# A Fourier tower's column transform with the data as stationary operand, its modes copied by ScalarE, layer 0 as a loop, and the ends of the layers in another order

## The chip, the cores and the metric

The kernel runs on one core of one Trainium2 chip. The metric is the device time of the whole program in microseconds, the median of several executions. The engines of the core are TensorE (PE: matmuls; PEld: its weight loads), VectorE (DVE), ScalarE (ACT), GpSimd (POOL) and SyncE (SP, which here only issues DMAs).

## The reference, cut to what matters

64 images of 64 x 64 tokens pass through a Fourier tower of four layers with 32 channels, then an attention block and a mixture of experts. The change touches the tower alone:

```python
x = coords @ fc0_w + fc0_b                       # 3 -> 32 channels
for sw, cw, cb in layers:                        # four layers
    x_ft = rfft2(x, norm='ortho')
    out = einsum('bixy,ioxy->boxy', x_ft[:, :, :20, :20], sw)   # 20 x 20 modes
    x1 = irfft2(out in a zeroed spectrum)
    x2 = einsum('bchw,oc->bohw', x, cw) + cb
    x = gelu(x1 + x2)
x = gelu(x @ fc1_w + fc1_b) @ fc2_w + fc2_b
```

## The kernel before, in words

The Fourier transforms are matmuls with small constant matrices, all in fp32. The images go through a layer in 32 pairs (`PAIRS`). For pair j of layer l, TensorE runs `step(l, j)`, in this order:

- `inverse_h(l, j + 1)` (line 541): the inverse column transform of the next pair, 8 matmuls of 64 x 64 weights and 320 columns, into PSUM banks 4 to 7;
- `conv(l, j)` (line 563): the 1 x 1 convolution, 16 matmuls of 32 x 32 and 512 columns, into banks 0 to 3;
- `inverse_w(l, j, 0)` (line 579): half of the inverse row transform, 32 matmuls of 64 x 64 and 64 columns, added onto banks 0 and 1;
- `dft_w` of pair j - 2 of the next layer (line 474): the forward row transform, 16 matmuls of 32 x 64 and 512 columns, into banks 4 to 7;
- `inverse_w(l, j, 1)`: the other half, onto banks 2 and 3;
- `dft_h` of pair j - 3 of the next layer (line 486): the forward column transform, 8 matmuls of 64 x 64 and 320 columns, into banks 0 and 1. Here the constant `fwd_h` is stationary and the data `turned_h` moves.

An fp32 matmul runs as two passes, each with a weight load and a matmul of its own in the trace, so 8 matmuls are 32 instructions. VectorE turns 32 x 32 blocks between the transforms: `turn_inverse` (line 776, two transposes of 1024 elements), `turn_act` (line 741, two), `turn_w` (line 752, two), `turn_modes` (line 766, one of 640) and `turn_h` (line 758, one of 640: out of `dft_h`'s banks into `modes`). That is also their order within a step: `turn_inverse(j + 1)`, `turn_act(j - 1)`, `turn_w(j - 2)`, `turn_modes(j + 3)`, `turn_h(j - 3)`. ScalarE applies the GELU to each half of the convolution's banks (line 890) and issues the store of the pair to HBM. SP loads the pair back for the next layer.

Banks 4 to 7 are used by `inverse_h` and by `dft_w`, so in each step `inverse_h`, `turn_inverse`, `dft_w` and `turn_w` follow one another, and the next `inverse_h` waits for `turn_w` (`take(w_turned, ...)`). `conv` waits for `turn_h` of pair j - 4, which frees banks 0 and 1.

Waits of TensorE inside a loop can only be on constants, so `steps` runs two steps a round and then takes off what the semaphores gained:

```python
with pe.Fori(0, rounds):
    for j in range(first, first + 2):
        step(l, j)
    for sem, count in used:
        give_back(sem, count)        # pe.nop().then_inc(sem, -count), line 460
```

`used` has nine semaphores in layers 1 and 2 and five in layer 3. Layer 0 is written out (`looped = 0`); in layers 1 and 2 pairs 4 to 29 run in 13 rounds. The line of the loop itself is 615.

After the last pair of a layer come the forward transforms still open (`ends`), with a few idle matmuls (`keep_busy`, line 569) between them, and then `mix(l)` (line 527), which multiplies all modes with the layer's spectral weights; it needs every pair's modes. Layer 0's spectrum is not made from the 32 channels but from the four input channels: for four groups of eight pairs, `dft_w`, `dft_h` and `turn_h` work on the input, and `lift` (line 504, copies on ScalarE at line 869) spreads it to the channels. Layer 0's convolution reads the input, which SP loads in four pieces of 1 MB (`xin`), with weights in `first_w`.

## Time and profile before

| | us |
|---|---|
| median of 3 executions | 1547.61 |
| lowest, highest | 1542.99, 1552.35 |
| the profiled execution | 1544.01 |
| its span on the core | 1542.2 |
| TensorE, weight loads, VectorE, ScalarE busy | 1369.6, 704.4, 1181.8, 532.8 |
| the tower's layers: first inverse transposes of layers 0, 1, 2, 3 | 65.67, 363.64, 660.58, 954.54 |

The busy time of TensorE counts each matmul from its start to a modelled end; several run side by side on tiles of the array, and the groups give the time in which at least one ran. An idle time stands before the group that ended it, with what released it; "issue" is time in which TensorE waited for nothing that the profile shows. The granted clock was the full one (1.00, 2.4 GHz) in all stretches of the pair loops.

### The profile page before, as it was taken

The page shows a single profiled execution, that of the slowest core. Times are in us where ns is not written, and L with a number is a line of the kernel's source. Part 1 is how long each engine was busy: PE and PEld are TensorE (multiplying, and loading weights), DVE is VectorE, ACT ScalarE, POOL GpSimd, SP SyncE. Part 2 cuts the span into 40 slices and gives each one's busy share as a digit, 9 for nine tenths or more (in the row PEclk, how much of TensorE's full clock was granted, in tenths as well). Part 3 has the DMA queues.
Part 4 walks back from the last instruction along what each step waited for, and adds up shares of the span by engine and source line. Part 5 has one row for each costly group of instructions (what it writes and reads, how often), then busy time and mean ns, then how long its engine had stood idle before and what let it go on. Part 6 is the DMA issues. An engine that isn't in the chain of part 4 may idle for free. (4 is left out here: it accounts for less than half of the span.)

```text
span 1542.2 us, 69028 instructions
## 1 busy us (share of the span) xinstructions
PE 1369.6 (89%) x32216; PEld 704.4 (46%) x32216; DVE 1181.8 (77%) x1433; ACT 532.8 (35%) x673; POOL 92.4 (6%) x45
## 2 busy tenths in 40 slices
PE   8888999997999999879999998778779998989996
PEld 3544444445444444544444445445531117853332
DVE  4499999997999999789999997555510007878886
ACT  2422222223222222222222222333359994421221
POOL 1000000000000000000000000000000000036551
PEclk9999999999999999999999999999999999999998
DMA  6324242346666666566666663899997751056420
GB/s 230 115 115 164 116 163 119 133 166 224 249 247 244 249 241 255 177 255 246 245 245 245 245 250 130 311 372 387 375 377 278 280 190 59 8 129 152 116 76 14
DMA packets 59934, 315.80 MB, mean 205 GB/s; under 512 B 16704, under 2 KB 18688, under 8 KB 25984
## 3 DMA queue, kind: packets, MB, share of 16 engines
q1 hardware_dynamic: 36512, 177.95, 34.0%
q10 hardware_dynamic: 23264, 135.49, 21.4%
q8 instruction: 130, 2.13, 0.6%
q14 instruction: 28, 0.23, 0.1%
HBM read 176.05 MB, written 137.36 MB: 203 GB/s over the span
## 5 line engine op out<-in xcount | busy, mean ns | idle before, releaser
L890 ACT ACTIVATE act_c<-slots,conv_b 128x1024 f32<-128x1024 f32 x256 | 282.1, 1115 | 717.8 <-PE slots L579 717.8
L776 DVE STREAM_TRANSPOSE inv_out<-slots 128x1024 f32<-128x1024 f32 x256 | 304.7, 1229 | 96.7 <-PE slots L541 96.7
L579 PEld LDWEIGHTS slots<-inv_w,inv_out 64*64 64x64 f32 x16384 | 270.7, 136 | 198.9 <-issue 188.7
L579 PE MATMUL slots<-inv_w,inv_out 64*64 64x64 f32 x16384 | 301.6, 224 | 14.7 <-issue 9.6
L752 DVE STREAM_TRANSPOSE turned_h<-slots 128x1024 f32<-128x1024 f32 x200 | 238.0, 1229 | 24.5 <-PE slots L474 24.4
L474 PE MATMUL slots<-turned_w,fwd_w 32*64 32x512 f32 x3200 | 201.5, 599 | 28.7 <-DVE inv_out L776 22.1
L741 DVE STREAM_TRANSPOSE turned_w<-act_c 128x1024 f32<-128x1024 f32 x192 | 225.6, 1218 | 0.8 <-ACTq L893 0.8
L541 PE MATMUL slots<-turned_k,inv_h 64*64 64x320 f32 x2048 | 169.3, 444 | 53.7 <-DVE turned_h L752 30.4
L563 PE MATMUL slots<-xin,conv_w 32*32 32x512 f32 x3072 | 112.7, 605 | 29.3 <-DMA xin<-act_scratch 17.6
L486 PE MATMUL slots<-turned_h,fwd_h 64*64 64x320 f32 x1600 | 132.7, 443 | 1.3 <-DVE turned_h L752 1.3
L541 PEld LDWEIGHTS slots<-turned_k,inv_h 64*64 64x64 f32 x2048 | 71.0, 133 | 131.1 <-DVE turned_h L752 76.5
L474 PEld LDWEIGHTS slots<-turned_w,fwd_w 32*64 32x64 f32 x3200 | 69.3, 131 | 90.1 <-issue 87.2
L766 DVE STREAM_TRANSPOSE turned_k<-modes 128x640 f32<-128x640 f32 x128 | 102.9, 807 | 0.5
L1781 POOL TENSOR_TENSOR modes<-at_turned,modes 128x1024 f32<-128x1024 f32 x6 | 14.4, 2394 | 1375.2 <-DMA at_turned<-level_scratch 1367.1
L901 ACT ACTIVATE inv_out<-slots,b 128x512 f32<-128x512 f32 x86 | 89.7, 1111 | 2.1 <-PE slots L698 2.1
L758 DVE STREAM_TRANSPOSE modes<-slots 128x640 f32<-128x640 f32 x96 | 77.5, 809 | 2.3 <-PE slots L486 2.3
L850 DVE TENSOR_SCALAR modes<-slots,b 128x512 f32<-128x512 f32 x4 | 3.0, 751 | 95.9 <-PE slots L710 95.9
L698 PE MATMUL slots<-act_c,w 32*64 32x512 f32 x1024 | 71.4, 612 | 3.9 <-ACT inv_out L901 1.8
L486 PEld LDWEIGHTS slots<-turned_h,fwd_h 64*64 64x64 f32 x1600 | 52.1, 132 | 35.4 <-issue 5.4
L563 PEld LDWEIGHTS slots<-xin,conv_w 32*32 32x32 f32 x3072 | 24.3, 103 | 80.5 <-DVE modes L758 34.9
L527 PE MATMUL slots<-modes,mode_w 64*64 64x128 f32 x1600 | 49.8, 271 | 6.3 <-issue 5.2
L800 DVE COPY modes<-slots 128x640 f32<-128x640 f32 x36 | 29.7, 825 | 33.2 <-PE slots L527 33.2
(166 smaller groups left out, 1116.8 us busy)
## 6 DMA issues: line engine op xcount, KB each, us to landing
act_scratch<-act_c ACTq DMA_DIRECT2D x128, 1024.0 KB, 4.2
xin<-act_scratch SPq DMA_DIRECT2D x96, 1024.0 KB, 4.8
act_c<-act_scratch SPq DMA_DIRECT2D x32, 1024.0 KB, 6.1
mode_w<-in_sw_dram SPq DMA_DIRECT2D x20, 640.0 KB, 4.3
at_turned<-level_scratch SPq DMA_DIRECT2D x24, 256.0 KB, 4.2
at_ret_t<-level_scratch SPq DMA_DIRECT2D x20, 256.0 KB, 4.2
xin<-in_x_dram SPq DMA_DIRECT2D x4, 1024.0 KB, 8.6
turned_w<-in_x_turned_dram SPq DMA_DIRECT2D x3, 1024.0 KB, 5.4
```

The costliest lines, as they stand in the source:

```text
L474: mm = nc.tensor.matmul(banks[i * 64:(i + 1) * 64, 4 + p, :], fwd_w[p * 32:(p + 1) * 32, wh, :], turned_w[p * 32:(p + 1) * 32, n % 2, wh, ...
L486: mm = nc.tensor.matmul(banks[kwh * 64:(kwh + 1) * 64, at + i, 0:320], fwd_h[i * 64:(i + 1) * 64, parity, ph, :], turned_h[i * 64:(i + 1) ...
L541: mm = nc.tensor.matmul(banks[s * 64:(s + 1) * 64, 4 + 2 * i + kwh, 0:320], inv_h[rows, l % 2, s * 64:(s + 1) * 64], turned_k[rows, t % 2, ...
L563: nc.tensor.matmul(banks[q * 32:(q + 1) * 32, p, :], w, src, start=True, stop=False, skip_group_check=True)
L579: mm = nc.tensor.matmul(banks[half * 64:(half + 1) * 64, 2 * two + odd, at:at + 64], inv_out[rows, t % 2, i, two, s, 2 * half:2 * half + 2 ...
L741: last = nc.vector.transpose(dst, src)
L752: nc.vector.transpose(dst, src).then_inc(w_turned, 1)
L758: nc.vector.transpose(dst, src).then_inc(modes_set, 1)
L766: nc.vector.transpose(dst, src).then_inc(modes_turned, 1)
L776: nc.vector.transpose(dst, src).then_inc(inv_turned, 1)
L890: nc.scalar.activation(act_c[:, t % RING, :, at, :].rearrange("p i q m -> p q i m"), banks[:, at, :].rearrange("p q (i m) -> p q i m", i=2 ...
L901: nc.scalar.activation(unit[n % 3][:, part, :], banks[:, at, :], ACT.Gelu, bias=b1[:, 0:1]).then_inc(unit_set, 1)
```

## The change

1. `dft_h` turns its operands round: the data (`turned_h`, 128 rows by 64 columns) is loaded as weights and the constant moves, 40 columns at a time. The constant now holds all 128 rows. The result comes out with the modes along the free dimension, so that it need not be transposed but only copied.
2. That copy is ScalarE's (`copy_modes`), behind the pair's second GELU and ahead of the store's issue; `turn_h` is gone from VectorE. At the start, `copy_first` is a copy on VectorE.
3. The layout of the modes changes with it: `mix_place` sets where each mode of the mixing goes, `inverse_h` becomes 16 matmuls of 32 x 64 weights and 320 columns that add up in pairs, `turn_inverse` reads all four banks for each image, and `lift` runs as 2 matmuls of 64 x 64 instead of 4 of 32 x 32. Host-made constants and the order of the spectral weights follow. The bytes loaded stay the same.
4. Layer 0 is looped like the others: the input comes in a piece for each pair (`load_x`, four DMAs of 32 KB), and `first_w` is the same for every pair. In layers 0 to 2 the loop runs over pairs 5 to 30.
5. At a layer's end `dft_w` of pair 29 comes ahead of the last `conv`; the last pair's activation is turned in two halves (`turn_last_act`), the first as soon as the first GELU is done; the last `dft_w` goes into banks 0 to 3 and the last two `dft_h` into banks 4 and 5 and 6 and 7.

```diff
@@ dft_w, dft_h
-            def dft_w(n):
+            def dft_w(n, at=4):
...
-                            mm = nc.tensor.matmul(banks[i * 64:(i + 1) * 64, 4 + p, :],
+                            g = i ^ p % 2
+                            mm = nc.tensor.matmul(banks[g * 64:(g + 1) * 64, at + 2 * i + p // 2, :],
...
-                for ph in range(2):
-                    take(w_turned, after_w_turned(n, ph))
-                    for i in range(2):
+                for i in range(2):
+                    take(w_turned, after_w_turned(n, i))
+                    for b in range(MIXES // 2):
                         for kwh in range(2):
-                            mm = nc.tensor.matmul(banks[kwh * 64:(kwh + 1) * 64, at + i, 0:320],
-                                                  fwd_h[i * 64:(i + 1) * 64, parity, ph, :],
-                                                  turned_h[i * 64:(i + 1) * 64, n % 2, ph,
-                                                           kwh * 320:(kwh + 1) * 320].rearrange(
-                                                      "p (b c m) -> p b m c", c=CH, m=2),
-                                                  start=(ph == 0), stop=(ph == 1))
+                            at_kw = kwh * 320 + b * 64
+                            mm = nc.tensor.matmul(
+                                banks[kwh * 64:(kwh + 1) * 64, at + i, b * 40:(b + 1) * 40],
+                                turned_h[:, n % 2, i, at_kw:at_kw + 64],
+                                fwd_h[:, i, parity, :].rearrange("p (k x) -> p k x", k=2)[:, :, 0:MODES],
+                                start=(b == 0), stop=True, skip_group_check=True)
@@ inverse_h
-                for i in range(2):
+                for odd in range(2):
                     for s in range(2):
-                        for kwh in range(2):
-                            rows = slice(kwh * 64, (kwh + 1) * 64)
-                            mm = nc.tensor.matmul(banks[s * 64:(s + 1) * 64, 4 + 2 * i + kwh, 0:320],
-                                                  inv_h[rows, l % 2, s * 64:(s + 1) * 64],
-                                                  turned_k[rows, t % 2, i * 320:(i + 1) * 320],
-                                                  start=True, stop=True)
+                        for r in range(4):
+                            rows = slice(r * 32, (r + 1) * 32)
+                            mm = nc.tensor.matmul(
+                                banks[s * 64:(s + 1) * 64, 4 + r, :].rearrange("p (i n) -> p i n", i=2)[:, :, 0:160],
+                                inv_h[rows, l % 2, odd, s * 64:(s + 1) * 64],
+                                turned_k[rows, t % 2, odd * 320:(odd + 1) * 320].rearrange("p (i n) -> p i n", i=2),
+                                start=(odd == 0), stop=(odd == 1))
@@ step
+                final = j == PAIRS - 1 and not last
+                if final:
+                    take(act_turned, after_turn(l + 1, j - 2))
+                    take(w_turned, after_w_turned(forward(l + 1, j - 3), 1))
+                    dft_w(forward(l + 1, j - 2))
@@ the layers of TensorE
-                first = 1 if last else 4
-                looped = 2 * ((PAIRS - 1 - first) // 2) if l > 0 else 0
+                first = 1 if last else 5
+                looped = 2 * ((PAIRS - 1 - first) // 2)
...
-                    dft_w(ends[1])
-                    take(act_high, after_set(l, PAIRS - 1))
-                    keep_busy(4, 3)
-                    dft_h(ends[0], parity, at=2)
-                    take(act_turned, after_turn(l + 1, PAIRS - 1))
-                    take(w_turned, after_w_turned(ends[1], 1))
-                    dft_w(ends[2])
-                    take(modes_set, ends[0])
-                    dft_h(ends[1], parity)
-                    take(modes_set, ends[0] + 1)
-                    dft_h(ends[2], parity, at=2)
-                    keep_busy(2, 4)
+                    dft_w(ends[2])
+                    take(act_low, after_set(l, PAIRS - 1))
+                    dft_h(ends[0], parity)
+                    take(act_high, after_set(l, PAIRS - 1))
+                    dft_h(ends[1], parity, at=2)
+                    take(act_turned, after_turn(l + 1, PAIRS - 1))
+                    take(modes_set, ends[1] + 1)
+                    dft_w(ends[3], at=0)
+                    dft_h(ends[2], parity, at=4)
+                    keep_busy(4, 7)
+                    dft_h(ends[3], parity, at=6)
+                    keep_busy(2, 0)
@@ VectorE
-                    if 3 <= j < PAIRS - 1:
-                        turn_h(forward(l + 1, j - 3), modes[:, 2 * (j - 3):2 * (j - 3) + 2])
                 if not last:
-                    turn_act(l + 1, PAIRS - 1)
+                    turn_last_act(l + 1)
                     turn_w(forward(l + 1, PAIRS - 2))
-                    for t in range(PAIRS - 4, PAIRS):
-                        if t == PAIRS - 2:
-                            turn_w(forward(l + 1, PAIRS - 1))
-                        turn_h(forward(l + 1, t), modes[:, 2 * t:2 * t + 2],
-                               at=2 if t in (PAIRS - 3, PAIRS - 1) else 0)
+                    turn_w(forward(l + 1, PAIRS - 1), at=0)
@@ ScalarE
+            def copy_modes(f, t, at=0):
+
+                act.wait_ge(h_done, forward(f, t) + 1)
+                nc.scalar.copy(modes[:, 2 * t:2 * t + 2, :, 0:MODES], modes_from(at)).then_inc(modes_set, 1)
...
+                        if two == 0 and t == PAIRS - 1 and l < LAYERS - 1:
+                            act.drain().then_inc(act_half, 1)
                     act.drain().then_inc(act_ready, 1)
+                    if t >= 3 and l < LAYERS - 1:
+                        copy_modes(l + 1, t - 3)
                     act.dma_start(act_dram[t], flat(act_c[:, t % RING])).then_inc(act_stored[t % RING], 16)
+                if l < LAYERS - 1:
+                    for t in range(PAIRS - 3, PAIRS):
+                        copy_modes(l + 1, t, at=2 * (t - PAIRS + 4))
@@ SP
+            def load_x(t):
+
+                if t >= IN_RING:
+                    sp.wait_ge(summed, after_out(0, t - IN_RING, 0))
+                for p in range(4):
+                    sp.dma_start(flat(xin[p * CH:p * CH + IN_CH, t % IN_RING]), x[t, p]).then_inc(
+                        xin_in[t % IN_RING], 16)
```

## Rows read from the trace of the kernel before

**Rows 1.** The page: span, busy time, the layers' GELUs.

```profile
PE 1369.6 (89%) x32216; PEld 704.4 (46%) x32216; DVE 1181.8 (77%) x1433; ACT 532.8 (35%) x673; POOL 92.4 (6%) x45
...
L890 ACT ACTIVATE act_c<-slots,conv_b 128x1024 f32<-128x1024 f32 x256 | 282.1, 1115 | 717.8 <-PE slots L579 717.8
```

**Rows 2.** Timeline, layer 1, one loop turn (start, us, engine, line, op).

```profile
504.39 1.31 PE L541 MATMUL slots<-turned_k,inv_h 64*64 64x320 f32 x16 [0.28 <-DVE turned_h L752]
504.99 0.81 DVE L758 STREAM_TRANSPOSE modes<-slots 128x640 f32<-128x640 f32 x1
505.76 2.38 DVE L776 STREAM_TRANSPOSE inv_out<-slots 128x1024 f32<-128x1024 f32 x2
...
508.07 2.34 DVE L741 STREAM_TRANSPOSE turned_w<-act_c 128x1024 f32<-128x1024 f32 x2
...
508.29 1.98 PE L474 MATMUL slots<-turned_w,fwd_w 32*64 32x512 f32 x32 [0.17 <-DVE inv_out L776]
...
510.20 1.05 PEld L579 LDWEIGHTS slots<-inv_w,inv_out 64*64 64x64 f32 x64 [0.81 <-issue]
...
510.36 2.38 DVE L752 STREAM_TRANSPOSE turned_h<-slots 128x1024 f32<-128x1024 f32 x2
511.15 0.78 PEld L486 LDWEIGHTS slots<-turned_h,fwd_h 64*64 64x64 f32 x16
...
513.04 1.31 PE L541 MATMUL slots<-turned_k,inv_h 64*64 64x320 f32 x16 [0.52 <-DVE turned_h L752]
...
514.41 2.38 DVE L776 STREAM_TRANSPOSE inv_out<-slots 128x1024 f32<-128x1024 f32 x2 [0.21 <-PE slots L541]
```

**Rows 3.** VectorE's timeline: inverse-transform transposes of layers 0 and 1.

```profile
133.08 2.38 DVE L776 STREAM_TRANSPOSE inv_out<-slots 128x1024 f32<-128x1024 f32 x2
...
142.87 2.38 DVE L776 STREAM_TRANSPOSE inv_out<-slots 128x1024 f32<-128x1024 f32 x2 [0.21 <-PE slots L541]
...
201.74 2.38 DVE L776 STREAM_TRANSPOSE inv_out<-slots 128x1024 f32<-128x1024 f32 x2
...
403.42 2.38 DVE L776 STREAM_TRANSPOSE inv_out<-slots 128x1024 f32<-128x1024 f32 x2
...
608.08 2.38 DVE L776 STREAM_TRANSPOSE inv_out<-slots 128x1024 f32<-128x1024 f32 x2
```

**Rows 4.** TensorE's sequencer at that loop turn: line 460.

```profile
L460 PEldq EVENT_SEMAPHORE  x9: 51/51/51, 511.2 to 512.4; - x9
```

**Rows 5.** Begun before a stretch's end: lines 579, 486 (PE, PEld xcount).

```profile
510.19:510.94 0.75, 0.75 (x48) 0.75 (x52) 1.00 1.00 426
...
510.94:511.18 0.24, 0.00 (x0) 0.03 (x4) 1.00 0.73 308
```

**Rows 6.** Timeline, later stage: loads of 128 rows by 64 columns.

```profile
1382.21 0.20 PEld L1267 LDWEIGHTS slots<-at_qkv,ex_lattice_w 128*64 128x64 f32 x4 [0.37 <-issue]
...
1383.12 0.14 PEld L1267 LDWEIGHTS slots<-at_centred_y,ex_lattice_w 128*64 128x64 f32 x2 [0.28 <-issue]
```

**Rows 7.** PE groups by form after 960 us: 128*128 and 128*64 forms.

```profile
L1210 PE MATMUL slots<-at_qkv,at_ret_t 128*128 128x64 f32 x64 | 7.9, 276 | 1.6 <-DVE at_ret_t L1418 1.6
```

**Rows 8.** DMA queue of instructions: 100 to 200 us, 400 to 500 us.

```profile
q8 instruction: 21, 0.34, 1.4%
...
q8 instruction: 2, 0.03, 0.2%
```

**Rows 9.** Timeline: end of layer 0 and start of layer 1's mixing.

```profile
326.50 2.38 DVE L752 STREAM_TRANSPOSE turned_h<-slots 128x1024 f32<-128x1024 f32 x2
...
336.26 2.33 DVE L741 STREAM_TRANSPOSE turned_w<-act_c 128x1024 f32<-128x1024 f32 x2
...
341.00 1.54 DVE L758 STREAM_TRANSPOSE modes<-slots 128x640 f32<-128x640 f32 x2
...
347.50 11.96 PE L527 MATMUL slots<-modes,mode_w 64*64 64x128 f32 x392 [0.33 <-DVE modes L758]
```

**Rows 10.** ScalarE's groups by form: the lift's copies.

```profile
L869 ACT COPY modes<-slots 128x400 f32<-128x400 f32 x32 | 15.8, 492 | 21.3 <-PE slots L504 21.3
```

More of the change, by code:

```diff
@@ L501, in lift @@
                     pe.wait_ge(first_w_set, 1)
-                for b in range(4):
-                    rows_b = slice(b * 32, (b + 1) * 32)
-                    mm = nc.tensor.matmul(banks[rows_b, 2 + n % 2, 0:400], lift_w[rows_b, e, :],
-                                          in_modes[rows_b, 2 * q:2 * q + 2, :, 0:MODES], start=True, stop=True)
+                for kwh in range(2):
+                    rows = slice(kwh * 64, (kwh + 1) * 64)
+                    mm = nc.tensor.matmul(banks[rows, 2 + n % 2, 0:400], lift_w[rows, e, :],
+                                          in_modes[rows, 2 * q:2 * q + 2, :, 0:MODES], start=True, stop=True)
                 mm.then_inc(lifted, 1)
@@ L629, in _ @@
             pe.wait_ge(fc0_cols_set, 1)
-            for e in range(LIFT_E):
-                mm = nc.tensor.matmul(banks[:, 3, e * CH:(e + 1) * CH], fc0_cols[:, e, :], conv_w[0:CH, 0, :],
-                                      start=True, stop=True)
-            mm.then_inc(first_w_filled, 1)
+            nc.tensor.matmul(banks[:, 3, 0:CH], fc0_cols, conv_w[0:CH, 0, :],
+                             start=True, stop=True).then_inc(first_w_filled, 1)
             warm_up(1)
@@ L714, in _ @@
             for _ in range(4):
-                nc.tensor.matmul(banks[:, 0, 0:128], inv_h[:, 0, :], inv_h[:, 0, :], start=True, stop=True)
+                nc.tensor.matmul(banks[:, 0, 0:128], inv_h[:, 0, 0, :], inv_h[:, 0, 0, :], start=True, stop=True)
         def mix_part(u, side, images=slice(0, IMAGES)):
-            k, half = u // 2 * 2 + side, u % 2
+            k, half = mix_place(u, side), u % 2
             dst = modes[:, images, k, half * 10:half * 10 + 10].rearrange("p i (m r) -> p i m r", r=2)
@@ L1825 @@
     fc0 = _np.concatenate([f[t + "fc0_w"], f[t + "fc0_b"][None, :]], axis=0)
+    for m in range(2):
+        lifted[:, :, :, m, :, m] = fc0
     wq, wk = f["L0_attn_W_Q"], f["L0_attn_W_K"]
```

153 lines of the change are left out of this document (87 added, 66 removed).

## The prediction

> **What bounds the kernel now.** The page first: TensorE is busy 89% of the span and VectorE 77%, ScalarE 35% [rows 1]. Both leaders are averages, so I went to the timeline of the pair loop, where layers 0 to 2 spend some 250 us each. One step there is a ring of four pieces that hand PSUM banks 4 to 7 to each other [rows 2]: `inverse_h` starts at 504.39; its two transposes (line 776) start 1.37 later, at 505.76, and last 2.38; `dft_w` follows at 508.29, that is 3.90 after the start, and lasts 1.98; its transposes (line 752) start at 510.36 and end at 512.74. If the next `inverse_h` came 0.05 later, the step would be 8.40 us. That is what layer 0, written out, shows: 142.87 to 201.74 is 7 steps, 8.41 each [rows 3]. VectorE's own list of a step comes to the same 8.41, since it has no gap in layer 0. So two limits of one size lie on each other, VectorE's list and the bank ring, and taking work from one alone wins nothing.
>
> In layers 1 and 2 TensorE runs a loop of two steps, and the mean is (608.08 - 403.42) / 24 = 8.53 [rows 3]: 8.41 and 8.65 in turn. The longer one is the loop's turn: `inverse_h` starts at 513.04, 0.30 after its transposes ended [rows 2]. The sequencer shows why. `give_back` makes nine semaphore decrements, the first at 511.2, 0.15 apart, then comes the branch, and the matmul starts 1.86 after the first decrement (511.18 to 513.04) [rows 2, 4]. When can that first decrement start? When line 579's half had 48 matmuls and 52 loads of 64 and 64 begun, the sequencer reached the wait behind it: 28 instructions stood queued. When `dft_h` had 4 loads of its 32 instructions begun, the first decrement came: 28 again [rows 5]. So the sequencer is held until the last 28 instructions before it are queued, and the decrements start only then. With today's `dft_h` that is right at its beginning.
>
> **The change part by part.** `dft_h` was 8 matmuls of 320 columns (16 loads and 16 matmuls, because each runs in two passes); it becomes 20 of 40 columns with 128 rows, so 40 loads and 40 matmuls on two column tiles. The trace has no such form. A second load on the same 128 by 64 tile comes 0.06 after the first (four loads in 0.20, two in 0.14) [rows 6], and line 579 with 16 loads on each of four tiles takes (1.05 - 0.14) / 15 = 0.06 a round [rows 2]. Twenty rounds make 1.21 us, against 1.31 for the 320-column form of the same size [rows 2]. The array's time hardly changes. The lower bound is line 579's rate over all tiles, 0.016 for each load, so 0.66; the upper one is that the two tiles don't run side by side, 2.42. I take 1.21, from the row with the same tile.
>
> The loop's turn pays. `dft_h` now has 80 instructions, and the first decrement must wait until 52 have gone: 52/80 of 1.21 = 0.79 after its first load. That load comes 3.90 + 1.91 + 0.95 = 6.76 after the step's start (508.29, 510.20, 511.15) [rows 2], and later by a change of tile shape, which was not there: 1.98 for 2048 columns and 1.31 for 1280 give 0.87 ns a column, so 1.79 for `dft_w`, while its successor starts after 1.91. I take 0.13 (bounds 0 and 0.2). Then 6.76 + 0.13 + 0.79 + 1.86 = 9.54 instead of 8.65: **+0.89 a turn**. Three layers have 13 rounds each: 39 x 0.89 = +34.7. The lower bound of the round gives 26 loads x 0.016 = 0.43, so +0.53 a turn and +20.7. In the other step `dft_h` ends at 6.76 + 0.18 + 1.21 + 0.17 (a last matmul's way out) = 8.32, just under the 8.40 of the ring; its cost there is nothing, but only 0.08 covers it.
>
> On the number queued, the trace shows 28 both times [rows 5]. The Trainium skill, "TensorE: Matmul & The Clock Gate", section Part 1, has TensorE's queue 64 deep; no row here shows that many waiting. By its 64 the turn would grow by 0.37 instead of 0.89; that case is a rival below.
>
> On loads: line 1210 has full 128-row loads, 64 of them with their matmuls in 7.9 us, 0.123 each [rows 7], less than a 128-column load at 0.06 for 64 (0.12) and 64 columns of matmul (0.05) one after the other. The same page, Part 3, says that a load overlaps a running matmul only where the row groups differ; by that `dft_h` would be serial, about 3.7 us, and the step longer than 10. The row of line 1210 speaks against it here.
>
> `inverse_h` becomes 16 matmuls on eight tiles with the same columns for each tile. `dft_w`, which has eight tiles, ends no later for it than the columns say; I take +0.02 on the ring for each of 93 steps, +2 (bounds 0 and 0.06 each). Waits and order of it are unchanged.
>
> Layer 0 becomes a loop. It gets 13 turns it did not have: 13 x 0.24 = +3.1 beside the 0.89 counted. It loses its three code stalls: 133.08 to 142.87 is 9.79 instead of 8.41 [rows 3], and two more of the kind cost 1.07 and 1.38: -3.8. The instruction queue fetched 21 times in 100 us of layer 0 and twice in 100 us of layer 1 [rows 8]. The input comes in four small DMAs a pair instead of a megabyte per eight pairs; each has two steps, 16.8 us, to land, and SP has nothing else to issue: nothing.
>
> The transpose of line 758, 0.81, leaves VectorE, 29 a layer in the stream [rows 2]. What hides it is the ring's 8.40; price nothing. VectorE then idles 0.7 a step while `inverse_h` runs. The end of a layer: from the end of line 752's transposes, 326.50 + 2.38 = 328.88, to mixing at 347.50 is 18.6 [rows 9]. Up to the last pair's turn (336.26) that was 7.4; with `dft_w` first it is 2.1 + conv 1.1 + two halves 2.2 + the last GELU 1.1 [rows 1] and handovers 0.2 = 6.7. From there it was 11.2; now a half turn 1.2 and a transposed pair 2.4, beside them two `dft_h` (2.5) and ScalarE's copies; `dft_w` into banks 0 to 3 ends 6.1 after the turn's start, its transposes at 8.5, the last half of `dft_h` 9.2, the copy 9.7. That is -0.7 - 1.5 = -2.2 a layer, -6.6 (bounds -3 and -10, for code stalls that move).
>
> ScalarE's copy of 400 elements takes 0.49, the lift's form [rows 10]. In the stream it starts once `dft_h` ends, 8.4, and ends at 8.9; `conv`, which waits for it, comes at 9.7. Behind it on ScalarE stand the store's issue, which is read a layer later, and a GELU due at 10.9: nothing. At the start four transposes become copies, at most 0.3 shorter each, partly hidden: -0.5; the wider lift weights fill an idle VectorE.
>
> Sum: +34.7 + 3.1 - 3.8 + 2.0 - 6.6 - 0.5 = **+28.9** on the profiled execution's 1544.0, so 1572.9; the median shown, 1547.6, is 3.6 higher, and I give 1576.
>
> **The rivals.** (a) The loop's turn does not lengthen, because the decrements start beside `dft_h` as they do now. Then only +3.1 - 3.8 + 2.0 - 6.6 - 0.5 = -5.8: 1542; with the smallest `inverse_h` and other code stalls gone too, 1536. This is the only way to faster, and it decides at the first decrement: it must stay within 0.1 of `dft_h`'s first load. The 28 queued speak against it; for it speaks that VectorE's list gets 9% shorter. 0.27, half of it faster. (b) The sequencer can run further ahead than the 28 seen, by 64: then 16 instructions of `dft_h` must be gone, 4 rounds, 0.24, so +0.37 a turn, 14.4 in all, and 1556. 0.09. (c) The two tiles of 128 rows don't run side by side: `dft_h` 2.42, the plain step 9.5, the turn 10.3, some +110: 1657. Against it speaks that two loads of this tile pair begin together [rows 6]. 0.05. (d) The loop's body, 528 instructions a step where it was 448, no longer stays in the instruction buffer and is fetched at each of 39 turns for about 1.2 us (the stalls of layer 0), +47: 1623. 0.06.
>
> **How the numbers follow.** The forecast has 0.53 with its own range 1560 to 1592, from the bounds of the round and of the ends. About 0.5% is what a measurement of this kernel tells from no change, 1540 to 1555. Faster is half of (a), 0.13; same the other half and little of (b), 0.14; slower 0.73. For 8 in 10, 1541 to 1602 leaves out part of (a), (c) and (d).
>
> **What would show it.** The loops' steps alternate 8.4 and 9.5; in the turn, the first decrement of line 460 comes 0.8 after `dft_h`'s first load; 28 instructions are queued then; `dft_h` lasts about 1.35; VectorE idles 0.7 a step; layer 0 has no code stall and the period of layers 1 and 2; each layer's end is 2 us shorter. If the turn stays at 8.65, the step on the queue is wrong, and the result is (a). If the plain step is over 8.5, the round is longer than 0.06.

## The result, and the profile after

The changed kernel takes 1610.3 us (1602.1 to 1614.8) where the kernel before took 1550.0 on the same chip: ratio 1.039, 95% interval 1.033 to 1.045, so +60 us. The forecast was 1576, range 1541 to 1602. The direction was right, and the time lies 8 us above the range. The profiled execution after takes 1610.4; that of before was a quick one (1544.0), so the two traces differ by 66 us, 6 more than the medians.

The page after (the span and busy rows, then the rows that answer to [rows 1] and the groups of the changed operations; lines 503, 516, 570, 593, 609 are `dft_w`, `dft_h`, `inverse_h`, `conv` and `inverse_w`, lines 773, 798, 811 and 821 `turn_act`, `turn_w`, `turn_modes` and `turn_inverse`, line 556 `mix`, line 911 `copy_modes`, line 488 `give_back`):

```profile
span 1608.6 us, 77928 instructions
PE 1418.4 (88%) x36522; PEld 826.4 (51%) x36522; DVE 1113.8 (69%) x1355; ACT 580.3 (36%) x769; POOL 92.3 (6%) x45
...
q8 instruction: 96, 1.57, 0.4%
...
L931 ACT ACTIVATE act_c<-slots,conv_b 128x1024 f32<-128x1024 f32 x256 | 282.2, 1114 | 714.2 <-PE slots L609 713.8
...
L570 PE MATMUL slots<-turned_k,inv_h 32*64 32x320 f32 x4096 | 182.5, 447 | 75.0 <-DVE turned_k L811 43.0
...
L516 PE MATMUL slots<-fwd_h,turned_h 128*64 128x40 f32 x4000 | 137.1, 230 | 3.5 <-issue 3.5
...
L911 ACT COPY modes<-slots 128x400 f32<-128x400 f32 x96 | 47.2, 492 | 41.8 <-PE slots L516 41.8
```

VectorE lost 68 us of work, as meant, and TensorE gained 49. To see where the time went, the two traces are cut at the same events: the first and the tenth inverse transpose (line 776 before, line 821 after) of a layer, its last one, and the first matmul of the mixing. The forecast is cut the same way from its own terms (it counts a turn's 0.89 or 1.13 in the stretch in which the turn lies):

| stretch, us | before | after | difference | forecast |
|---|---|---|---|---|
| start to the mixing of layer 0 | 47.8 | 50.4 | +2.6 | -0.5 |
| the four mixings, first matmul to first inverse transpose | 66.1 | 75.7 | +9.6 | 0 |
| first to tenth inverse transpose, layers 0, 1, 2 | 67.4, 65.5, 65.3 | 71.9, 77.0, 77.1 | +27.8 | +3.0 |
| tenth to last, layers 0, 1, 2 | 188.8, 187.5, 187.4 | 197.3, 198.5, 198.8 | +30.9 | +29.5 |
| last to the next mixing, three ends | 25.6, 27.7, 25.5 | 25.4, 24.4, 24.4 | -4.7 | -3.1 |
| from layer 3's first inverse transpose on | 587.7 | 587.7 | 0 | 0 |

The loops, the ends and the last layer came as priced. Two stretches did not: the mixing, which the forecast did not look at, and the first nine steps of a layer, most of which are written out. The timeline of one loop turn after, layer 1 (start, us, engine, line, operation), against [rows 2]:

```profile
500.34 1.19 PE L609 MATMUL slots<-inv_w,inv_out 64*64 64x64 f32 x64
...
501.46 1.25 PEld L516 LDWEIGHTS slots<-fwd_h,turned_h 128*64 128x64 f32 x40
501.46 1.36 PE L516 MATMUL slots<-fwd_h,turned_h 128*64 128x40 f32 x40
...
503.91 1.46 PE L570 MATMUL slots<-turned_k,inv_h 32*64 32x320 f32 x32 [1.09 <-DVE turned_k L811]
...
505.45 2.38 DVE L821 STREAM_TRANSPOSE inv_out<-slots 128x1024 f32<-128x1024 f32 x2 [1.84 <-PE slots L570]
...
507.98 1.98 PE L503 MATMUL slots<-turned_w,fwd_w 32*64 32x512 f32 x32 [0.39 <-DVE inv_out L821]
...
510.05 2.38 DVE L798 STREAM_TRANSPOSE turned_h<-slots 128x1024 f32<-128x1024 f32 x2
511.01 1.25 PEld L516 LDWEIGHTS slots<-fwd_h,turned_h 128*64 128x64 f32 x40
511.01 1.36 PE L516 MATMUL slots<-fwd_h,turned_h 128*64 128x40 f32 x40
...
512.42 0.49 ACT L911 COPY modes<-slots 128x400 f32<-128x400 f32 x1 [0.15 <-PE slots L516]
512.49 1.34 PE L570 MATMUL slots<-turned_k,inv_h 32*64 32x320 f32 x32
```

At 501.46 `dft_h` starts; `inverse_h` comes 2.45 later, at 503.91, though its banks were free at 502.88 (line 798 from 500.50 for 2.38). That is 1.03 behind the banks, where the plain step's `inverse_h` is 0.06 behind them (512.49 against 510.05 + 2.38): the turn is 0.97 late, and the rest of its extra 1.1 is the longer `inverse_h` (1.46 instead of 1.34). In the plain step `dft_h` (511.01 + 1.36 = 512.37) is done 0.12 before the ring lets `inverse_h` start, at 512.49. From 503.91 to 512.49 is 8.58, the step after a turn; the transposes of line 821 stand 8.48 and 9.6 apart in turn. The sequencer's decrements of that turn (count, ns, first and last start):

```profile
L488 PEldq EVENT_SEMAPHORE  x9: 51/51/51, 502.1 to 503.3; - x9
```

And `dft_h`'s matmuls and loads begun up to the first of them:

```profile
core 0: us, PE busy (x) PEld busy (x), PEclk, DMA share, GB/s
501.45:502.08 0.63, 0.62 (x22) 0.62 (x22) 1.00 1.07 455
```

The first comes 0.62 after `dft_h`'s first load, with 22 loads and 22 matmuls of 80 begun: 36 stand queued, not the 28 of [rows 5]. From it to `inverse_h` are 1.83, as before (1.86).

### The profile page after: what moved, and what is told of

It is laid out like the page before. It is cut to its first block and busy times, and to the rows that moved or that the text cites. A ratio compares the mean times of both kernels' runs of the same rounds, so it can differ in the third digit from the quotient of the medians.

```text
span 1608.6 us, 77928 instructions
## 1 busy us (share of the span) xinstructions
PE 1418.4 (88%) x36522; PEld 826.4 (51%) x36522; DVE 1113.8 (69%) x1355; ACT 580.3 (36%) x769; POOL 92.3 (6%) x45
## 5 line engine op out<-in xcount | busy, mean ns | idle before, releaser
L570 PE MATMUL slots<-turned_k,inv_h 32*64 32x320 f32 x4096 | 182.5, 447 | 75.0 <-DVE turned_k L811 43.0
L503 PE MATMUL slots<-turned_w,fwd_w 32*64 32x512 f32 x3200 | 206.9, 606 | 44.6 <-DVE inv_out L821 31.9
L773 DVE STREAM_TRANSPOSE turned_w<-act_c 128x1024 f32<-128x1024 f32 x186 | 218.7, 1216 | 0.0
L570 PEld LDWEIGHTS slots<-turned_k,inv_h 32*64 32x64 f32 x4096 | 88.6, 133 | 110.6 <-PEq L488 43.9
L516 PE MATMUL slots<-fwd_h,turned_h 128*64 128x40 f32 x4000 | 137.1, 230 | 3.5 <-issue 3.5
L516 PEld LDWEIGHTS slots<-fwd_h,turned_h 128*64 128x64 f32 x4000 | 125.4, 138 | 18.5 <-issue 12.5
L593 PE MATMUL slots<-xin,conv_w 32*32 32x512 f32 x3072 | 113.5, 605 | 19.5 <-DMA xin<-act_scratch 17.7
L556 PE MATMUL slots<-modes,mode_w 64*64 64x128 f32 x1600 | 64.9, 300 | 0.6 <-issue 0.6
L556 PEld LDWEIGHTS slots<-modes,mode_w 64*64 64x64 f32 x1600 | 63.9, 136 | 1.8 <-issue 1.3
L911 ACT COPY modes<-slots 128x400 f32<-128x400 f32 x96 | 47.2, 492 | 41.8 <-PE slots L516 41.8
```

The lines of the kernel that those rows point to most:

```text
L503: mm = nc.tensor.matmul(banks[g * 64:(g + 1) * 64, at + 2 * i + p // 2, :], fwd_w[p * 32:(p + 1) * 32, wh, :], turned_w[p * 32:(p + 1) * 3 ...
L516: mm = nc.tensor.matmul(banks[kwh * 64:(kwh + 1) * 64, at + i, b * 40:(b + 1) * 40], turned_h[:, n % 2, i, at_kw:at_kw + 64], fwd_h[:, i, ...
L556: mm = nc.tensor.matmul(mix_sums(rows_to, side, u % 2)[:, m * 128:(m + 1) * 128], mode_w[rows, n % RING_W, side, kh, :], modes[rows, :, k, ...
L570: mm = nc.tensor.matmul(banks[s * 64:(s + 1) * 64, 4 + r, :].rearrange("p (i n) -> p i n", i=2)[:, :, 0:160], inv_h[rows, l % 2, odd, s * ...
L593: nc.tensor.matmul(banks[q * 32:(q + 1) * 32, p, :], w, src, start=True, stop=False, skip_group_check=True)
L773: last = nc.vector.transpose(dst, src)
```

## The experiments

The table names three suspects: the loop turn, the mixing, and code that comes late in the written-out steps. On the last of them two theories stood. **A**: 528 instructions a step come too slowly whenever they run for the first time, whatever the traffic. **B**: they come late only beside the activations' megabyte transfers. The first seven kernels take one part out of the changed kernel or put one part into the kernel before. In several of them the numbers computed are not the transform's; they are for timing alone. Each ratio is to the kernel before, timed again beside that run (1547.2 to 1550.3); differences in us are between medians, and are good to some 5 to 10.

**dft_h_back**: the changed kernel with `dft_h` of 8 matmuls of 320 columns.

```diff
-                    for b in range(MIXES // 2):
+                    for r in range(2):
                         for kwh in range(2):
...
-                                turned_h[:, n % 2, i, at_kw:at_kw + 64],
-                                fwd_h[:, i, parity, :].rearrange("p (k x) -> p k x", k=2)[:, :, 0:MODES],
...
+                                fwd_h[r * 64:(r + 1) * 64, i, parity, :],
+                                turned_h[r * 64:(r + 1) * 64, n % 2, i, kwh * 320:(kwh + 1) * 320]...,
...
```

> The changed kernel with dft_h back at 8 matmuls of 64x64 weights and 320 columns; everything else of the change stays (the modes that come out are not the transform's). Theory (the queue before the loop's turn): the turn falls from 9.5 us to about 8.65, 39 of them, some -34 us, and the code stalls of the written-out steps shrink too, since a step has 48 instructions fewer; 1550 to 1570 in all. Rival (dft_h costs nothing, all of the loss is in the mixing and the code stalls): over 1595, the turn stays near 9.5.

Measured 1572.9 us, ratio 1.016 (1.010 to 1.021), 3 above the range expected. The steps of layers 1 and 2 are 8.48 and 8.71; tenth to last transpose takes 190.7, 189.1 and 188.9 instead of 197.3, 198.5 and 198.8, so 26 us come back there, and 15 in the first nine steps. `dft_h`'s new form is the larger half of the loss (37 of 60 us).

**dft_h_alone**: the kernel before with 20 such matmuls of 64 columns in `dft_h`.

```diff
-                    for i in range(2):
+                    for b in range(MIXES // 2):
                         for kwh in range(2):
...
-                                                  fwd_h[i * 64:(i + 1) * 64, parity, ph, :],
-                                                  turned_h[i * 64:(i + 1) * 64, n % 2, ph, ...
...
+                                turned_h[:, n % 2, ph, at_kw:at_kw + 64],
+                                fwd_h[:, parity, ph, :],
...
```

> The kernel before with dft_h alone in the new form: 20 matmuls with 128x64 weights from the data, 64 columns each here so that turn_h finds its banks filled (the values are not the transform's). Layer 0 stays written out. Theory (the sequencer's nine decrements start only once most of dft_h has gone): 26 turns at 9.4 to 9.5 us instead of 8.65, plain steps at 8.41 to 8.5, some +22 us, and code stalls on top in written-out steps, above all layer 0's 32: 1575 to 1610. Rival (dft_h's array time is what costs): plain steps grow too, by over 0.3 us each.

Measured 1568.1, ratio 1.010 (1.006 to 1.015), less than the 1575 to 1610 expected. Steps 9.43 and 8.41 in layers 1 and 2, where the loop is, and mostly 8.41 in layer 0, where there was none, though `dft_h` lasts 1.39 there: its array time costs nothing, the turn pays. Layer 0's stalls grow a little (tenth to last transpose 193.5 against 188.8). At the turns 34 instructions stand queued.

**inverse_h_alone**: the kernel before with `inverse_h` of 16 matmuls.

```diff
-                for i in range(2):
+                for odd in range(2):
                     for s in range(2):
-                        for kwh in range(2):
-                            rows = slice(kwh * 64, (kwh + 1) * 64)
-                            mm = nc.tensor.matmul(banks[s * 64:(s + 1) * 64, 4 + 2 * i + kwh, 0:320],
...
+                        for r in range(4):
+                            rows = slice(r * 32, (r + 1) * 32)
+                            mm = nc.tensor.matmul(banks[s * 64:(s + 1) * 64, 4 + r, :]...[:, :, 0:160],
...
```

> The kernel before with inverse_h alone as 16 matmuls of 32x64 weights (values not the transform's). Theory: it ends 0.03 later and lies on the ring of banks 4 to 7, so plain steps take 8.44 to 8.48 instead of 8.41, +3 to +7 us. Rival: hidden, no change.

Measured 1565.0, ratio 1.010 (1.008 to 1.013): +16, where 3 to 7 were expected. The plain step is 8.47, so `inverse_h` costs the ring 0.06, my upper bound, not 0.02. The rest is not the ring's: the first nine steps of a layer lose 8.6 us in the trace (206.8 for three layers, against 198.2), most of it in stalls of written-out steps, which have 32 instructions more. A turn grows to 8.7 or 8.96; in such a one it also lasts 1.59, where the plain step has 1.34. Its timeline, a turn and a plain step:

```profile
506.51 1.59 PE L541 MATMUL slots<-turned_k,inv_h 32*64 32x320 f32 x32 [0.53 <-DVE turned_h L753]
...
515.23 1.34 PE L541 MATMUL slots<-turned_k,inv_h 32*64 32x320 f32 x32 [0.28 <-DVE turned_h L753]
```

**mix_undone** (places and targets of the mixing as before), **mix_tiles** (the targets alone) and **mix_alone** (the kernel before with the changed places and targets). The change had put into `mix`:

```diff
+            block, odd = (2 * (u // 4) + side, u // 2 % 2) if u < 8 else (4, side)   # mix_place
+            return 2 * block + odd
...
-                                to = kwh ^ side
-                                k, kh = u // 2 * 2 + side, u % 2 * 5 + m
+                                k, kh = mix_place(u, side), u % 2 * 5 + m
+                                to = kwh ^ k // 2 % 2
```

In steps 8 and 9 `k // 2 % 2` is 0 for both sides, so their matmuls use two of the four 64 by 64 tiles. In steps 0 to 7 all four are used, but the two sides read modes two places apart, not side by side.

> The changed kernel with the mixing's places as before: the two sides read neighbouring places (k, k+1), and all ten steps use four tiles (the modes then belong to other weights). Theory (the mixing lost its speed by where the two sides read and by the two-tile steps): a mixing step takes 1.10 to 1.27 us again instead of 1.45 and 2.18, some -4 us a layer, 1590 to 1597. Rival (the mixing waits for the copies or for its code): the steps stay at 1.45, no change from 1610.

> The changed kernel with only the tiles of the mixing's last two steps as before, four instead of two. If the two-tile steps alone were the loss, all of -16 us comes back; the theory says that only their part does: 2.18 to about 1.2 us for two steps a layer, -8 us at most, and the eight others stay at 1.45 us, since their two sides read places two apart.

> The kernel before with the changed kernel's places and tiles in the mixing alone (modes then meet other weights). Theory: mixing steps 1.45 and 2.18 us instead of 1.10 to 1.27, +16 us. Rival (the slower mixing came from another part of the change): no change.

Measured: mix_undone 1598.3, ratio 1.032 (1.024 to 1.040); mix_tiles 1604.1, 1.035 (1.029 to 1.041); mix_alone 1558.3, 1.006 (1.003 to 1.008). The intervals are wide for differences of 6 to 12 us; the traces are sharper. Per layer the mixing lasts 18.9 in the changed kernel and in mix_alone, 16.9 in mix_tiles, and 15.7 to 16.8 in mix_undone. VectorE's copies behind the last four steps of the mixing, layer 1, changed kernel:

```profile
374.38 0.82 DVE L844 COPY modes<-slots 128x640 f32<-128x640 f32 x1 [0.62 <-PE slots L556]
375.84 0.82 DVE L844 COPY modes<-slots 128x640 f32<-128x640 f32 x1 [0.63 <-PE slots L556]
378.00 0.82 DVE L844 COPY modes<-slots 128x640 f32<-128x640 f32 x1 [1.34 <-PE slots L556]
380.19 0.20 DVE L846 COPY modes<-slots 128x40 f32<-128x40 f32 x1 [1.37 <-PE slots L556]
```

The same four in mix_tiles:

```profile
373.41 0.82 DVE L844 COPY modes<-slots 128x640 f32<-128x640 f32 x1 [0.64 <-PE slots L556]
374.86 0.82 DVE L844 COPY modes<-slots 128x640 f32<-128x640 f32 x1 [0.63 <-PE slots L556]
375.97 0.82 DVE L844 COPY modes<-slots 128x640 f32<-128x640 f32 x1 [0.28 <-PE slots L556]
377.23 0.20 DVE L846 COPY modes<-slots 128x40 f32<-128x40 f32 x1 [0.43 <-PE slots L556]
```

A step on two tiles takes 2.16 or 2.19, on four tiles 1.11 or 1.26: 2.0 a layer. And a four-tile step whose sides read places two apart takes 1.46 (374.38 to 375.84). The matmuls of a stretch of such steps in the changed kernel (count, then shortest, median and longest in ns):

```profile
L556 PE MATMUL slots<-modes,mode_w x287: 287/308/319, 364.7 to 375.0; 64*64 64x128 f32 x144
```

And those of the kernel before:

```profile
L527 PE MATMUL slots<-modes,mode_w x238: 266/267/323, 348.8 to 356.0; 64*64 64x128 f32 x119
```

With the places restored too (mix_undone) the median is 267 again, while mix_tiles, which has the old tiles and the new places, stays at 307. The two differ in the places alone, so it is the places that slow the matmuls; by what mechanism was not tried. Eight steps at 1.45 instead of 1.10 and 1.27 would be 2.1 a layer, but mix_undone gains only some 0.7 over mix_tiles: the quicker mixing has 5.4 us of idle put to "issue" in its four mixings, the changed kernel's has 0.6 and the kernel before 5.2. In the traces the four mixings of mix_undone are 10.7 us shorter than the changed kernel's.

**layer0_written_out**: the changed kernel with `looped = 0` in layer 0.

```diff
-                looped = 2 * ((PAIRS - 1 - first) // 2)
+                looped = 2 * ((PAIRS - 1 - first) // 2) if l > 0 else 0
```

> The changed kernel with layer 0 written out as in the kernel before. The 13 turns at 9.45 us become plain steps of 8.48, -12.6 us. Theory A (the code of 528 instructions a step comes too slowly whenever it runs for the first time): stalls of 0.5 to 2 us in most steps eat that up, 1605 to 1630. Theory B (the stalls need the 1 MB loads of layers 1 and 2 beside the stores): layer 0's steps run at 8.48 with few stalls, about 1598.

Measured 1606.8, ratio 1.041 (1.034 to 1.047): no difference that its few runs can tell. In the trace layer 0 has steps of 8.48 and 8.59 without turns, and still tenth to last takes 195.1 against 197.3. 22 steps of 8.48 would be 186.6: written out, they lose 8.5 in stalls, nearly what the loop loses in turns (10.7). That is theory A's time, and against theory B in the form expected here, which needs the loads of layers 1 and 2: layer 0 has the stores alone, and its written-out steps stall all the same.

**quarter_traffic** decides between the two: the changed kernel with a quarter of the bytes of the activations stored and loaded, but for layer 3's stores and the first pairs, which stay whole.

```diff
-                sp.dma_start(flat(xin[:, t % IN_RING]), act_dram[t])...
+                n = 2048 if l == 1 and t < IN_RING else 512
+                sp.dma_start(flat(xin[:, t % IN_RING])[:, 0:n], act_dram[t][:, 0:n])...
...
-                    act.dma_start(act_dram[t], flat(act_c[:, t % RING]))...
+                    n = 2048 if l == LAYERS - 1 or l == 0 and t < IN_RING else 512
+                    act.dma_start(act_dram[t][:, 0:n], flat(act_c[:, t % RING])[:, 0:n])...
```

> The changed kernel with a quarter of the activations stored and loaded in layers 0 to 2 (the rest is not stored, so later layers compute with old values). Theory B (code pages wait behind the 1 MB transfers): the written-out steps and the first round of the loop in layers 1 and 2 fall from 8.9 to 13 us towards 8.5, and their 20 us come back: 1590 or below. Theory A (pages are asked for too late whatever the traffic): the stalls stay, 1605 or above.

Measured 1577.4, ratio 1.017 (1.013 to 1.021): -33 us, as theory B has it; theory A had 1605 or above. The loop steps stay at 8.47 and 9.6. The first nine steps of layers 1 and 2 fall from 77.0 and 77.1 to 67.5 and 68.5, those of layer 0 from 71.9 to 70.8. Late code shows as idle time in which TensorE waited for nothing else ("issue"), or for its sequencer. Those rows of TensorE's timeline from 420 to 455 us, in the first steps of layer 1, changed kernel (two more, of 1.21 and 0.60, lie at 396.02 and 400.42):

```profile
420.83 1.93 PE L503 MATMUL slots<-turned_w,fwd_w 32*64 32x512 f32 x19 [0.46 <-issue]
431.51 1.97 PE L503 MATMUL slots<-turned_w,fwd_w 32*64 32x512 f32 x30 [0.93 <-issue]
...
445.77 0.72 PE L516 MATMUL slots<-fwd_h,turned_h 128*64 128x40 f32 x17 [1.58 <-issue]
447.85 2.72 PE L570 MATMUL slots<-turned_k,inv_h 32*64 32x320 f32 x32 [1.36 <-PEq L488]
```

With a quarter of the bytes the same stretch has one such row, and no row in either waits for a DMA:

```profile
432.63 0.35 PE L610 MATMUL slots<-inv_w,inv_out 64*64 64x64 f32 x8 [0.49 <-issue]
```

What the queue of instructions fetched from 383 to 460 us (packets, MB, share) in the changed kernel:

```profile
q8 instruction: 14, 0.23, 1.1%
```

And in quarter_traffic:

```profile
q8 instruction: 13, 0.21, 1.3%
```

The same code is fetched, and nearly nobody waits for it. That the stalls are late code can be read from the packets of q8: in the changed kernel each of the eleven stalls over 0.4 us put to "issue" in the first steps of layers 1 and 2 ends 1.27 to 1.44 after one of them has landed, though they come 3.5 to 7.2 apart. So do the kernel before's at 139.9 and 208.0 in layer 0 (1.49 and 1.45). What the trace does not show is where a fetch loses its time. The packets themselves take no longer beside the full transfers (median 0.98, and 1.06 with a quarter of the bytes), so the delay lies ahead of the packet, and that it waits behind the transfers is not shown. Nor is it the traffic alone. The kernel before fetched five packets from 388 to 407 us with the DMA engines 0.66 busy and had no such stall there; the changed kernel's share from 412 to 443 was 0.53. The longer step counts too: the first nine steps of layers 1 and 2 take 65.3 and 65.5 with 448 instructions a step, 67.4 to 72.1 with 480 or 496 (dft_h_back, inverse_h_alone, dft_h_alone), and 77.0 and 77.1 with 528.

Behind the stall at 445.77 TensorE's granted clock falls to its lower level, 1.2 GHz, for 6.8 us, and line 570 lasts 2.72 instead of 1.34; in layer 2 it falls at the same place, for 3.4. The window of that stretch (the granted clock is the third figure from the end, 0.54):

```profile
446.00:452.80 6.80, 5.44 (x93) 2.58 (x93) 2.15 (x2) 0.49 (x1) 0.00 (x0) 0.54 0.39 157
```

But layer 3 also became 13 us shorter, which has nothing to do with the change, so a control was needed. **quarter_before** is the same edit in the kernel before.

> The kernel before, with a quarter of the activations' bytes stored and loaded in layers 0 to 2 (the rest of each activation is left out, so the numbers are others). The control for quarter_traffic. Theory B (code pages wait behind the megabyte transfers, and only the longer code of the changed kernel suffers from it): here the written-out steps of layers 1 and 2 are already 65.4 from the first to the tenth inverse transpose and have 0 to 1 us to lose, and what falls is layer 3's store-bound part, -13 us as in quarter_traffic, so 1548 - 14 = 1534 (1530 to 1537), ratio 0.991. Rival (the traffic slows the pair loops of both kernels by a general tax): the first ten transposes of layers 1 and 2 fall by 5 us or more here too, and the time is 1525 or less.

Measured 1524.0, ratio 0.983 (0.980 to 0.986): -25, more than expected, and its time is where I had put the rival. The trace does not say the rival's: the first nine steps of layers 1 and 2 fall by only 0.6 and 0.5, from 65.5 and 65.3, not by 5. What fell is layer 3 (tenth to last 122.3 to 108.7), and layer 0, whose written-out steps go from 188.8 to 185.0, that is 22 times 8.41: the code stalls that [rows 3] show at 142.87 are gone in the kernel before too. Up to layer 3's first inverse transpose the two kernels gain 19.5 and 5.6 us in their traces, so 14 us are the change's own; by the medians it is 33 - 25 = 8. The control also shows that stores alone are enough to make code late: layer 0 loads no activation, and its stalls went with the stores' bytes.

**spread_before** and **spread_after** test the turn itself, without touching `dft_h`: six of the nine decrements are made ahead of the second step's `dft_w`, after their last use in the round.

```diff
+                    for sem, count in early or []:
+                        give_back(sem, count)
...
                     take(inv_turned, after_inv_turned(l, j + 1, 1))
                     dft_w(forward(l + 1, j - 2))
...
+                    late = [(inv_turned, 4), (act_low, 2), (w_turned, 4)] if l < LAYERS - 1 else used
+                    early = [x for x in used if x not in late]
+                    step(l, first)
+                    step(l, first + 1, early)
+                    for sem, count in late:
```

> The changed kernel with the same six decrements moved. Theory (the nine decrements behind dft_h's queue make the turn): six of them are 0.9 us, so the turn falls from 9.5 to 8.6, 39 x 0.9 = -35 us, about 1575. Rival: the turn is set by dft_h's array time, and stays over 9.2.

> The kernel before with six of the nine decrements of a round moved ahead of the second step's dft_w, where TensorE waits for VectorE anyway; three stay at the turn. Theory: the turn falls from 8.65 to the ring's 8.41 in layers 1 and 2, 26 x 0.24 = -6 us, 1542. Rival (the six hold back dft_w instead): the second step grows by as much, no gain or a loss.

Measured: spread_after 1574.1, ratio 1.016 (1.012 to 1.020), so -36 with every instruction of `dft_h` in place; its turns are 8.57 in layer 0 and 8.76 to 8.80 in layers 1 and 2. spread_before 1546.2, ratio 0.999 (0.997 to 1.002), no gain, and its turn stays at 8.65. Its timeline over one turn tells why: `inverse_h` is on time (idle 0.28, the plain step's), but now `dft_w` is 0.25 late (0.42 instead of the 0.17 of [rows 2]).

```profile
506.34 1.31 PE L541 MATMUL slots<-turned_k,inv_h 64*64 64x320 f32 x16 [0.28 <-DVE turned_h L756]
...
510.49 1.98 PE L474 MATMUL slots<-turned_w,fwd_w 32*64 32x512 f32 x32 [0.42 <-DVE inv_out L780]
...
515.00 1.31 PE L541 MATMUL slots<-turned_k,inv_h 64*64 64x320 f32 x16 [0.28 <-DVE turned_h L756]
```

Both places lie on the ring. Six early decrements are 6 x 0.15 = 0.9, too many for the first, nine too many for the second. **three_early_before** moves three (the edit against spread_before).

```diff
-                    late = [(inv_turned, 4), (act_low, 2), (w_turned, 4)] if l < LAYERS - 1 else used
-                    early = [x for x in used if x not in late]
+                    early = used[3:5] + used[6:7] if l < LAYERS - 1 else []
+                    late = [x for x in used if x not in early]
```

> The kernel before, with three of the nine decrements of a loop turn (not six) moved ahead of the second step's dft_w, in layers 1 and 2. In spread_before the six delayed that dft_w by 0.25 us, which is as much as the turn had cost, so nothing was won. Theory (the sequencer has about 0.6 us of slack ahead of dft_w and lacks 0.24 at the turn; a decrement costs 0.15): three early ones, 0.45, fit into the first and free the second, so the steps of layers 1 and 2 alternate 8.41 and 8.41 and the time falls by 26 x 0.24 = 6 us: ratio 0.996, 1542. Rival (splitting the decrements has a price of its own wherever they stand): the step stays at 8.6 or more and the ratio is 1.000.

Measured 1539.8, ratio 0.994 (0.992 to 0.996), 11 runs: 0.6% below the kernel before, a small gain but clear of the noise. The turn is 8.33, even shorter than the plain step, since `dft_w` now starts 0.05 after line 780 is done, not 0.15 as in [rows 2], and so in every round from 430 us on. Its timeline:

```profile
506.72 2.38 DVE L780 STREAM_TRANSPOSE inv_out<-slots 128x1024 f32<-128x1024 f32 x2
...
509.15 1.98 PE L474 MATMUL slots<-turned_w,fwd_w 32*64 32x512 f32 x32
...
513.67 1.31 PE L541 MATMUL slots<-turned_k,inv_h 64*64 64x320 f32 x16 [0.29 <-DVE turned_h L756]
```

**three_causes_out** takes all three costs out of the changed kernel together (the edits of spread_after, mix_undone and quarter_traffic).

> The changed kernel with all three suspected costs taken out together: six decrements moved ahead of the second step's dft_w (spread_after, -36 alone), the mixing's places and tiles as in the kernel before (mix_undone, -12 alone), and a quarter of the activations' bytes in layers 0 to 2 (quarter_traffic, -33 alone, of which some 14 are layer 3's and fall in the kernel before as well). What the mixing computes and what is stored differ from the reference. Theory (the three causes are separate and add up): 1610 - 36 - 12 - 33 = 1529 (1524 to 1535), which is at or below quarter_before, so nothing of the 60 us is left unexplained. Rival (they overlap, because one late step hides another): 1540 or more.

Measured 1528.9, ratio 0.988 (0.984 to 0.991). The terms add up: 1610.3 - 36.2 - 11.9 - 32.9 = 1529.3. That they do so to half a microsecond is luck, since each is known to some 5 to 10 only. Against quarter_before, 1524.0, 4.9 us of the 60 are left; the two intervals overlap. It is a net sum: in the traces the first nine steps are still 7.2 us longer and the later ones 6.4, and the shorter ends give back 6.3 and the mixing 2.9.

## Why the prediction was wrong

**Right: the turn.** This was the largest term, and the runs carry it as a mechanism: spread_after gave back 36 us (some 5 either way) against the 34.7 forecast for all 39 turns, though it takes out six decrements of nine and not the wait for `dft_h`, so the two need not be equal. The steps inside it were off in ways that cancelled. 36 instructions stand queued, not 28, so the first decrement comes 0.62 after `dft_h`'s first load and not 0.79; the change of tile shape costs `dft_h` 0.17 (500.34 to 501.46 is 1.12, against 0.95 before) and not 0.13; the decrements cost what they did; and `inverse_h` runs longer in a turn. The 64 of the Trainium skill, "TensorE: Matmul & The Clock Gate", section Part 1, is not reached here either, though 36 is nearer to it; rival (b) is out. `dft_h`'s length, 1.36 against 1.21 + 0.17 forecast, rules out rival (c), and with it the serial reading of Part 3 of the same page: 40 loads in the same row groups take 1.25 beside their matmuls. Rivals (a) and (d), as they were written, are out too: the turn did lengthen, and the loop's body is not fetched again (q8 has no packet from 455 to 640 us, over ten rounds of layer 1). Two slips in the prediction's sums change nothing: the plain step takes 0.18 for the change of tile shape where the turn takes 0.13, and rival (b)'s 8.99 is 0.34 over 8.65, not 0.37. The last matmul's way out, 0.17, stood on no row; the changed kernel shows 1.36 - 1.25 = 0.11.

**Right: layer 0. Right in its sum alone: the ends.** Layer 0's 22 later steps were forecast at 11 x 1.13 + 22 x 0.02 - 3.8 = +9.1 and came at +8.5. The three ends are -4.7 with their exit turns, forecast -3.1, but not by the steps I gave, so that is luck: the last pair's `dft_w` waits for two `dft_h` and then for ScalarE's copy, which I had put beside it. The changed kernel's timeline there:

```profile
354.47 2.53 PE L516 MATMUL slots<-fwd_h,turned_h 128*64 128x40 f32 x80
...
357.05 0.49 ACT L911 COPY modes<-slots 128x400 f32<-128x400 f32 x1 [0.67 <-PE slots L516]
357.69 1.98 PE L503 MATMUL slots<-turned_w,fwd_w 32*64 32x512 f32 x32 [0.68 <-ACT modes L911]
```

It ends 7.6 after the last turn's start (352.07), not 6.1. In layer 0's end alone, 0.2 was gained, and 3.4 in layer 1's, where the kernel before had lost 2.2 more than in its neighbours; 2.2 less a turn, 1.1 each, was forecast.

**Wrong, 1: the mixing stood at nothing** because it was not looked at. The prediction lists what `mix_place` does only as a layout. The diff changes `to` and `k` in `mix`, and working the formula through for u = 8 and 9 would have shown two tiles instead of four: +2.0 a layer. The rest, 0.4 a layer, is from the distance of the places, net of the idle time put to "issue" that it covers; no row of before shows it. In all +9.6, and 12 by mix_undone's medians.

**Wrong, 2: layers 1 and 2 have code stalls in their written-out steps, and I priced code only in layer 0 and in rival (d)'s loop.** [Rows 8] were read as a rate over layer 1's loop (2 fetches in 100 us), and the nine steps ahead of it passed as 8.4 each. They were nearly that before, with 448 instructions a step and four of them ahead of the loop, not five. With 528, and a megabyte stored and one loaded per step, code comes late again and again, for 0.4 to 1.7 us, once in each of the two layers with the lower clock behind it. That is +24.8 beyond the forecast in this stretch, of which the traffic experiment takes back 19.1 (1.1, 9.5 and 8.5), less 1.4 that it also takes from the kernel before. Of the 5.7 that are left, 2.1 is layer 0's first step, 6.90 against 4.77: the granted clock was at its lower level from 71.0 to 77.8 there, and before only from 63.4 to 66.8, ahead of it. Some 1.3 is the longer `inverse_h`; the rest was not traced. The Trainium skill, "Runtime: NRT & Kernel Launch", section on instruction fetch mechanics, has each engine's next page fetched ahead by a DMA queue of its own, and hidden by the pace at which instructions are issued. That code comes by a queue of its own is what the packets above show; that it is hidden holds for layers 1 and 2 of the kernel before and nearly so with a quarter of the traffic, and not for the changed kernel.

**Wrong, 3, small: `inverse_h`.** 0.02 a step was taken, 0.07 measured (line 570's start to line 821's is 1.44, [rows 2] 1.37): +4 to +5 over 93 steps. That is at the upper bound of 0.06 or just over it.

**Open.** How the transfers delay a fetch, and how the distance of the places slows a matmul. 2.6 us at the start: the stretch up to the first mixing varies between 47.2 and 52.5 among these kernels, so nothing can be said of it. And of the late code, 8 us by the medians (33 - 25) and 14 to 18 by the traces are the change's own; which is nearer these few runs do not settle.

## What to carry to other kernels

Price an instruction count twice: where it runs, and in front of everything the sequencer must still do. Work behind a queue of 30-odd small matmuls (a loop's bookkeeping, here nine decrements of 0.15) starts late by their number, and spreading that work to a place with slack gave back more than half of the loss (36 of 60 us); look for the slack first, since in the kernel before six decrements moved were as bad as none and three were right. Written-out code can come late: here steps of 528 instructions next to heavy transfers stalled where steps of 448 did not, although the queue fetches little. And a new layout changes every loop that indexes by it: write out which tiles it uses for the last values of its index.

## What the runs showed of the hardware

- The sequencer stood 28 instructions ahead with `inverse_w` and the 8-matmul `dft_h` [rows 5], 36 with the 20-matmul form on two tiles, and 34 when that form has 64 columns instead of 40 (dft_h_alone). The number queued is not one constant.
- Where the mixing's two sides read modes two places apart, a matmul takes 308 ns instead of 267, and a load 137 instead of 130.
- Each stall of TensorE's written-out steps over 0.4 us that nothing else explains ended 1.2 to 1.6 us after a 16 KB packet of code had landed (layers 0 to 2 of the kernel before, the changed kernel and seven others). The packets of code took no longer beside four times the traffic.
- With three decrements ahead of it, `dft_w` started 0.05 after the transposes that it waits for, and without them 0.15 after (three_early_before against [rows 2]), in all of layer 1's later rounds; with six it started 0.39 after (spread_before). Why the wait ends sooner was not tried.
